# A four-layer graph kernel: first tile of each attention step searched from its bare guess, one adjacency product moved into the step change, side pairs over other rounds

## The reference

```python
for s in range(STEPS):                      # 2 steps
    A = _adj_from_feats(Xa, W1, W2, W3)     # softmax, nucleus 0.9, softmax again
    Xf = Rf @ Xf
    Xb = Rb @ Xb
    Xa = A @ Xa
    Z = Z + (Xf @ U1[s] + Xb @ U2[s] + Xa @ U3[s])
```

## Time and profile before

| | |
|---|---|
| median of 3 runs | 3476.09 us (3475.62 to 3479.3) |
| the profiled execution | 3477.54 us |
| its span | 3475.8 us |
| TensorE busy, granted clock | 3141.6 us (90%), 0.958 |
| VectorE busy | 2449.9 us (70%) |
| ScalarE busy | 1598.2 us (46%) |
| POOL busy | 2154.7 us (62%) |
| exact-loop rounds (MAX8) | 74 |

### The profile page before, as it was taken

One profiled execution on the slowest core, in us unless ns is written; L12 is line 12 of the kernel. 1 busy time (PEld: TensorE's weight loads), 2 busy tenths in 40 slices (PEclk: granted clock), 3 DMA queues, 4 the chain that ended last, 5 costly groups with the idle time before them and its releaser, 6 DMA issues. The chain is left out here.

```text
span 3475.8 us, 42043 instructions
## 1 busy us (share of the span) xinstructions
PE 3141.6 (90%) x13212; PEld 2270.6 (65%) x13212; DVE 2449.9 (70%) x3401; ACT 1598.2 (46%) x2357; POOL 2154.7 (62%) x4214
## 2 busy tenths in 40 slices
PE   4999989997799999999976689988899999996899
PEld 3888778885567777777754255544566666664788
DVE  6840123333998889888883799999988999998000
ACT  2311322225666666666653445545555555652100
POOL 2212421114788888888881677878988788886211
PEclk9999999998899999999988899999999999998899
DMA  7644344433112222122111111211222222233255
GB/s 254 241 146 145 116 151 167 165 130 87 44 54 59 61 63 60 57 60 64 57 37 58 47 56 53 57 48 51 58 82 75 78 80 82 74 87 99 96 197 173
DMA packets 140702, 327.59 MB, mean 94 GB/s; under 512 B 15456, under 2 KB 93664, under 8 KB 129248
## 3 DMA queue, kind: packets, MB, share of 16 engines
q1 hardware_dynamic: 140512, 325.30, 29.5%
HBM read 286.70 MB, written 38.54 MB: 94 GB/s over the span
## 5 line engine op out<-in xcount | busy, mean ns | idle before, releaser
L1025 ACT ACTIVATE junk<-E,negp 128x3327 uint8<-128x3327 f32 x208 | 637.3, 3064 | 141.3 <-issue 107.3
L1397 DVE SCALAR_TENSOR_TENSOR U<-E,trial 128x3327 f32<-128x3327 f32 x182 | 678.1, 3726 | 0.0
L920 PE MATMUL bank<-big,adj 128*128 128x512 f32 x1352 | 608.7, 601 | 8.7 <-ACT t L1051 8.7
L920 PEld LDWEIGHTS bank<-big,adj 128*128 128x128 f32 x1352 | 252.4, 192 | 328.9 <-issue 327.9
L297 PE MATMUL bank<-big,E 128*128 128x256 f32 x1664 | 366.7, 382 | 2.8 <-PEq L58 1.7
L880 PE MATMUL bank<-Hc,PT 128*128 128x256 f32 x1248 | 303.1, 395 | 65.5 <-ACT PT L1064 65.4
L880 PE MATMUL bank<-Hc,adj 128*128 128x256 f32 x1456 | 338.0, 384 | 16.4 <-ACT adj L1064 16.2
L297 PEld LDWEIGHTS bank<-big,E 128*128 128x128 f32 x1664 | 315.8, 191 | 50.3 <-issue 5.7
L1359 DVE TENSOR_REDUCE nmax<-E 128x1 f32<-128x3327 f32 x52 | 188.0, 3615 | 208.8 <-ACT E L1068 208.8
L880 PEld LDWEIGHTS bank<-Hc,adj 128*128 128x128 f32 x1456 | 279.5, 193 | 79.8 <-issue 22.5
L880 PEld LDWEIGHTS bank<-Hc,PT 128*128 128x128 f32 x1248 | 244.3, 198 | 126.3 <-ACT PT L1064 77.0
(11 more groups left out here) (248 smaller groups left out, 5750.2 us busy)
## 6 DMA issues: line engine op xcount, KB each, us to landing
adj<-adjT SPq DMA_DIRECT2D x131, 448.0 KB, 3.4
E<-adjT SPq DMA_DIRECT2D x32, 1664.0 KB, 6.9
adj<-adjT SPq DMA_DIRECT2D x104, 384.0 KB, 3.3
adj<-adjT SPq DMA_DIRECT2D x20, 1664.0 KB, 7.0
E<-adjT SPq DMA_DIRECT2D x26, 1216.0 KB, 5.8
xt<-xin SPq DMA_DIRECT2D x52, 128.0 KB, 5.8
x_d<-xn SPq DMA_DIRECT2D x52, 128.0 KB, 1.7
xt<-x_d SPq DMA_DIRECT2D x52, 128.0 KB, 5.3
```

Source lines behind the costliest of these rows:

```text
L920: last = mm(agg[:, 0:w], adj[:, SPAN * (k % 2) + j - AGG[k]], rhs[:, j], start=(j == 0), stop=False)
L1025: go(junk[:, 0:N], E[:, t % DEPTH, 0:N], func, bias=negp[:, t % 2, j:j + 1], scale=1.0, accum_out=acc_[:, t % 2, j:j + 1]).then_inc(summed ...
L1397: V_.scalar_tensor_tensor(out=U[:, 0:N], in0=e, scalar=point, in1=e, op0=ALU.is_ge, op1=ALU.mult, accum_out=found))
```

## The change

Four things change.

1. Tiles 0 and 26 (`unaided(t)`: t % NT == 0) have no ScalarE passes and no POOL updates. The guess, without the shift, is written as the first point at once and `bracketed` is raised. VectorE searches the tile right behind the next tile's maximum, a round earlier than the others, with 4 evaluations in step one and 5 in step two (`ALONE`). ScalarE's first copy of the tile after next waits for `bracketed` there, since that copy's sums overwrite what the guess reads.
2. `KEEP_END` of step two is 0.85 instead of 0.75, for all its tiles.
3. Step two's first product stands in round 27, the others in round n + 5 (LATE = 5): rounds 32 to 56. In rounds in which scores are made and nothing is turned (`filling`: 0 to 3 and 31 to 34), all four parts of the product come behind the four slots.
4. The 13 side pairs stand in rounds 45 to 48, 50 to 52 and 54 to 59 (`PAIRS`). Where a round has no product, SP loads both blocks of the pair itself; the loads for the last layer stay in round 59 (CLOSE = 7).

```diff
@@ -17,6 +17,7 @@
 EVALS = (3, 4)
+ALONE = (4, 5)
...
-KEEP_END = (0.8, 0.75)
+KEEP_END = (0.8, 0.85)
...
-LATE = 7
+LATE = 5
+CLOSE = 7
+PAIRS = (0, 1, 2, 3, 5, 6, 7, 9, 10, 11, 12, 13, 14)
...
-            side_at = lambda i: i - (NT + LAG + FIRST + 7) if 0 <= i - (NT + LAG + FIRST + 7) < NT // 2 else None
+            side_at = lambda i: PAIRS.index(i - (NT + LAG + FIRST + 7)) if i - (NT + LAG + FIRST + 7) in PAIRS else None
...
+            unaided = lambda t: t % NT == 0
+            aided = lambda t: t - 1 - t // (NT + 1)
...
-            agg_at = lambda i: i if 0 <= i < NT else i - LATE if NT <= i - LATE < tiles else None
+            agg_at = lambda i: i if 0 <= i < NT else NT if i == NT + 1 else i - LATE if NT < i - LATE < tiles else None
...
-            spread = [b for i in range(rounds + 1) for b in [last_at(i)] if b is not None and i < tiles + LATE]
+            spread = [b for i in range(rounds + 1) for b in [last_at(i)] if b is not None and i < tiles + CLOSE]
...
+                        def load_side(v, k):
+                            to = SPAN * k
+                            sp.dma_start(adj[:, to:to + FIRST], adjT[2 * v + k, :, 0:FIRST]).then_inc(side_in[k], 16)
...
                             if v is not None:
+                                if n is None:
+                                    for k in range(2):
+                                        load_side(v, k)
                                 for k in range(2):
                                     sp.wait_ge(side_done[k], v + 1)
-                                    load_chunk(n + 1, k)
-                            if i == tiles + LATE:
+                                    if n is not None and n + 1 < tiles:
+                                        load_chunk(n + 1, k)
+                            if i == tiles + CLOSE:
...
+                            filling = L is not None and T is None
...
-                                if n is not None:
+                                if n is not None and not filling:
+                                    neighbours(n, k)
+                            if n is not None and filling:
+                                for k in range(SLOTS):
                                     neighbours(n, k)
...
                                     act.wait_ge(lg_done, SLOTS * L + k + 1)
+                                    if k == 0 and L >= 2 and unaided(L - 2):
+                                        act.wait_ge(bracketed, L - 1)
...
-                                if k == 0 and R is not None:
+                                if k == 0 and R is not None and not unaided(R):
                                     sums(R, 1, 0)
...
-                                 ts(ga_(8), ga_(5), 1.0, -SHIFT[step], ALU.mult, ALU.add))
+                                 ts(ga_(8), ga_(5), 1.0, 0.0 if unaided(t) else -SHIFT[step], ALU.mult, ALU.add))
...
-                            offer(t, 0)
+                            if not unaided(t):
+                                offer(t, 0)
...
-                            prepare(t)
+                            if unaided(t):
+                                then(ts(trial2[:, d, POINT:POINT + 1], p, 1.0, None, ALU.mult))
+                                pool.sem_inc(bracketed, 1)
+                            else:
+                                prepare(t)
...
-                            for k in range(EVALS[step]):
+                            for k in range(ALONE[step] if unaided(t) else EVALS[step]):
...
                             if F is not None:
                                 row_max(F)
-                            if S is not None:
+                                if unaided(F - 1):
+                                    find(F - 1)
+                            if S is not None and not unaided(S):
                                 find(S)
```

More of the change, by code:

```diff
@@ L820, in _ @@
                                     elif v is not None:
-                                        to = SPAN * (k - 2)
-                                        sp.dma_start(adj[:, to:to + FIRST],
-                                                     adjT[2 * v + k - 2, :, 0:FIRST]).then_inc(side_in[k - 2], 16)
+                                        load_side(v, k - 2)
                                     elif n + 1 < tiles:
@@ L1015, in sums @@
                         def sums(t, j, m):
+                            a = aided(t)
                             if m == 0:
-                                act.wait_ge(aimed[j], t + 1)
+                                act.wait_ge(aimed[j], a + 1)
                                 if j > 0:
-                                    act.wait_ge(summed[j - 1], PASSES[j - 1] * (t + 1))
-                                elif t >= 1:
-                                    act.wait_ge(summed[1], 2 * t)
+                                    act.wait_ge(summed[j - 1], PASSES[j - 1] * (a + 1))
+                                elif a >= 1:
+                                    act.wait_ge(summed[1], 2 * a)
                             else:
-                                act.wait_ge(summed[j], 2 * t + 1)
+                                act.wait_ge(summed[j], 2 * a + 1)
                             func, acc_ = ((ACT.Relu, over), (ACT.Sign, sign))[m]
@@ L1099, in _ @@
                                         go(h3o[:, W % 2], dense[:, 0:D], ACT.Copy).then_inc(h3_copied, 1)
-                                if k == 3 and F is not None:
+                                if k == 3 and F is not None and not unaided(F):
                                     sums(F, 0, 1)
@@ L1123, in _ @@
                                         go(junk_y[:], y[:, X % 2], ACT.Copy, accum_out=stat[:, X % 2, 0:1]).then_inc(ln_a, 1)
-                                    if R is not None:
+                                    if R is not None and not unaided(R):
                                         sums(R, 1, 1)
@@ L1140, in _ @@
                                            accum_out=stat[:, X % 2, 2:3]).then_inc(ln_a, 1)
-                                    if F is not None:
+                                    if F is not None and not unaided(F):
                                         sums(F, 0, 0)
@@ L1245, in update @@
                             count, mass_ = up_(5 + j), up_(8 + j)
-                            pool.wait_ge(summed[j], PASSES[j] * (t + 1))
+                            pool.wait_ge(summed[j], PASSES[j] * (aided(t) + 1))
                             then(ts(count, sign[:, q, j:j + 1], 0.5, N / 2, ALU.mult, ALU.add))
```

## The result

| | before | after |
|---|---|---|
| median (5 runs each) | 3475.75 us (3473.58 to 3479.3) | 3491.74 us (3488.35 to 3494.7) |
| the profiled execution | 3477.54 us | 3493.73 us |
| its span | 3475.8 us | 3491.9 us |
| exact-loop rounds (MAX8) | 74 | 72 |

The ratio of the times is 1.0046, with a 95% interval from 1.0035 to 1.0057: slower, by less than half a percent. The forecast was 3466 us; the time lies inside the range (3433 to 3493), on the other side of no change.

A forecast was written before the change was run, and what follows sets the result against it. TensorE was taken to bound step one and 2434.7 to 3083, VectorE step two's first half and the last searches. 3477.54 + 6 + 0 + 4 - 20 = 3467.5, less 1.45 to the median: 3466 us; range over cases 3433 to 3493.

The forecast's parts named there:

- Part one: Fill of step one: search 0 starts earlier, search 1 5.4 us later, TensorE 6.2 later; +6, carried to step one's end.
- Part four: TensorE-bound stretch and drain: fewer pairs, earlier end of products and less idling give some -20; last search ends near 3196.
- signs of being wrong: MAX8 not 74 in all; search 1 earlier than 895; turn 26 before 1995; round 28 ending past 1862.
- The extra 12 of round 45: First round with a side pair, 12 us over: a stall that may stay or go, taken as 6, bounds 0 and 12.
- The 3.6 us that VectorE idles before search 51: In the drain: this idling goes, since the round feeding that bracket has no product any more; 3.6 us gained.
- The two pairs' 8: Rounds 49 and 53: leaving out two pairs before round 57 gives TensorE 10.2 us, of which about 8 remains.
- Parts two and three: Step change, product in round 27: 0, bounds +5 and -3. Fill of step two: search 28 4 us later, +4.
- Factor 0.85: Step two's searches: costs nothing itself, direction of the 45 rounds unknown; taken as 0, bounds 19 rounds fewer or as many more.
- Rival 1: Tiles 0 and 26 and the new factor: bare guesses cost extra exact-loop rounds, 8.9 us each; three more give 3493; chance 0.23.
- Rival 2: Step two's searches: the factor saves exact-loop rounds, three fewer in all, giving 3439; chance 0.22.
- Rival 3: Step two: all TensorE's moved work comes off, two rounds' products (48.8) and two pairs (10.2), giving 3417; chance 0.04.
- Rival 4: Nothing is left: round 45's 12 us stay and the step change costs its 5, giving 3477; chance 0.08.

The follow-up runs named there:

- e4: Kernel before with only the moved products (27, 32 to 56) and the change's side pairs: 3479.82 us against 3475.88, ratio 1.0012.
- e10: Kernel before plus bare searches with tile t+2's maximum inside, factor 0.85, products in rounds n + 6 (26 in 27), old pairs: 3431.97 us against 3475.81.
- e12: e10 with the change's rounds for the side pairs as the only edit: 3433.93 us against 3476.93, ratio 0.9876 to the kernel before.
- e3: Kernel before with the factor 0.85 alone: 3469.18 us against 3475.88, ratio 0.9977.
- e2: Kernel before with the fill order alone (rounds 0 to 3, 33, 34: score slots first, then the product): 3487.48 us against 3475.88.
- e8: Kernel before with product 26 in round 27, the others in rounds n + 6, side pairs as before: 3474.17 us against 3479.63.
- e6: Kernel before with bare searches alone, tile t+2's maximum taken inside the bare search: 3446.08 us against 3479.63, ratio 0.9904.
- e1: Kernel before with the bare searches of tiles 0 and 26 alone: 3481.45 us against 3475.88, ratio 1.0019.
- e7: e2 plus three unread matmuls behind each of the first three score slots of rounds 0 to 3: 3487.89 us against the kernel before's 3479.63.

## Why the prediction was wrong

**What held.** Search 26 starts 28 us earlier against its surroundings (1905 for 1932.68 predicted: 27.7), and its search ends 21.8 earlier (22.5). Search 27 gains 3.3 (3; the count of 21 us from exponential to search that Part one makes gives 1990 and a gain of 1.6, so the match is partly luck). Less the 12.8 of step one, the turn of tile 26 is at 2006.7 (2006), and search 28 3.8 late (4). Exponential 2 started after 875 and right behind search 0. MAX8 is 72, not 74, one of the signs of being wrong; so is the end of round 28 (turn 25 at 1867.07, where 1862 was the limit), which is step one's loss carried on. (Part four's 3196 for the end of the last search leaves out step one's +6; the sum has it.)

**Part four: predicted -20, measured -2.8** (from +19.6 to +16.8). This step is 17 of the 26 us by which the forecast missed. What failed in it is the premise that from 2434.7 to 3083 TensorE sets the pace, read from busy shares of 632.7 and 599.4 in 648.3 us. VectorE's waits for other engines in the kernel before, over that window, are (us in total, times, longest)

```profile
DVE nmax L1359 <- ACT E L1068: 24.4, 4, 10.3
...
DVE sc L1395 <- POOLq L1274: 0.6, 1, 0.6
```

and the last of the four is

```profile
2624.32 3.62 DVE L1359 TENSOR_REDUCE nmax<-E 128x1 f32<-128x3327 f32 x1 [6.38 <-ACT E L1068]
```

From there to the end of search 50 at 3160 the searches stand back to back on VectorE. Work taken from TensorE in rounds 49 and 53 can't end them earlier, and e4 shows it: turn 49 comes 8 us less late, search 49 only 0.7. In its own terms:

- *The extra 12 of round 45, taken at 6.* It is 61.1 us as before (2498.46 to 2559.53), and the 8.72 us wait for `t L1067` is in it. The row of it was already in the earlier trace rows ("8.7 <-ACT t L1051 8.7"): ScalarE's copy that frees the bank stands behind a normalisation copy, which waits for a POOL result. It is 8.7 in all fourteen kernels. The prediction saw a shift of 4 us "against POOL and ScalarE", but everything came to that round shifted together (turn 36, with which it starts, and search 37, beside it, are both 19.6 late here, and equal to within 0.1 us in every kernel), so nothing acted on this wait, and it was the bound 0 that held. Whether a shift of one engine against the others would remove it wasn't tried.
- *The 3.6 us that VectorE idles before search 51 "go".* They went, and 7.83 us in front of search 50 took their place (at 3136.03, above). POOL's timeline there:

```profile
3111.53 4.10 POOL L1318 TENSOR_TENSOR xn<-xn 128x256 f32<-128x256 f32 x1
...
3118.34 0.57 POOL L1231 TENSOR_TENSOR ga<-Zs,known 128x1 f32<-128x1 f32 x1
...
3124.79 3.48 POOL L1251 TENSOR_SCALAR trial<-trial 128x1 f32<-128x1 f32 x1
...
3135.51 0.33 POOL L1296 TENSOR_SCALAR trial<-up,ends 128x1 f32<-128x1 f32 x1
```

  The bracket stands behind the whole guess of tile 51 and the layer norm's steps on POOL, which are nearly back to back from 3105.86 to 3136.03. That round has no product in it here, while e10 has one there and waits 3.05 us at the same place, so the product, which the prediction blamed for such a wait, is not what this one hangs on: it grows as search 49 comes earlier (e12 against e10). In e4, where search 49 comes only 0.7 us less late than search 44, the 3.6 us shrink to 1.0 and no other wait takes their place.
- *The two pairs' 8.* On TensorE they were right: the turn of tile 49 goes from +19.4, at tile 41, to +8.9. Search 49 followed with +6.2, but only because the factor had left VectorE room: of the 13.4 us that it gains on search 44, 8.4 are there in e3 too, without the pairs, and in e4, without the factor, it gains 0.7. Search 50 then waits for POOL, and the gain ends there. In this kernel tile 50 also has one round more by the factor (8.9). e12, with both kernels at two rounds there, shows the pairs' worth alone: nothing.

**Part one: predicted +6, measured +12.8,** of which 2.1 come before the first scores. The step that failed is "it needs maximum 1 (starts 827.37)": the same part lets TensorE's rounds grow from 19.6 to 25, yet kept that maximum's start. It is 5.7 late. Behind it the count on ScalarE was nearly right: from exponential 2 to search 1 21 us were predicted (880 to 901) and 22.8 measured. The second and third fill rounds are 27.6 and 27.3 us, not 25, and on their own (e2) delay search 0 by 15.3: the fill order was the largest single loss of the four, and the prediction gave it no line of its own.

**Parts two and three: predicted 0 and +4.** The turn of tile 25 has +2.4 over step one's share, inside the bounds of +5 and -3. Step two's fill gave 3.8 at search 28 and 3 more by search 30: together 6.8.

**Factor 0.85: predicted 0, measured -7** (e3). Its bounds held, and its rounds fell by two. In the whole change the one that paid in e3, tile 27's, lies in the 14.40 us that VectorE waits for maximum 30 and saves nothing.

**Rivals.** Rival 1 gave 3493 and the measured time is 3491.74, but by another cause: MAX8 fell, so the guesses were not dear. Rival 2 was right in direction and saw its saving inside the loss. Rival 3's mechanism, all of TensorE's moved work coming off, is not borne out: e12 shows no gain by the pairs, e4 a loss. The Trainium skill (Perfetto Trace Analysis, "Identifying Performance Opportunities") says that interleaving regimes with different busiest engines may help; the runs agree only for the move by one round (e8: -2.5 at the last search), while the move by two with the pairs gave +3.9. Rival 4 came nearest to what Part four did.

**What the prediction missed** is how large that one sentence was ("maximum 2 now stands behind that search"). It priced the delay as a side effect to bear, against a gain of 16 to 28 us on the search, and didn't ask what the change would be without it: e6 against e1.

## What to carry to other kernels

When a long operation is moved forward on an in-order engine, list what it now stands in front of, and for the shortest of these that feeds another engine look for a place inside the long one; here a 3.6 us maximum, twice, was worth 35 us. Two engines can both be over 90% busy in a stretch: which one sets the pace is read from who still waits for another there, not from the larger share. A wait doesn't change by a shift that all engines share; before counting on its going, name the engine that moves against the others. A gain on one engine near a drain ends at the next wait for another queue, so follow it to the last instruction before it goes into the sum.

## What the runs showed of the hardware

POOL's small operations stretch beside one kind of VectorE pass. The operation over 128x1 at 3124.79 took 3.48 us where its like take 0.19 to 0.57, and it ended with VectorE's pass over two inputs (L1467, 3124.59 for 3.61); the operation at 3111.53 took 4.10 instead of 0.73, beside VectorE's cut (L1427, 3110.83 for 4.22). While VectorE ran MAX8 and MATCH_REPLACE, from 3115.89 to 3124.29, POOL did 21 operations of 0.19 to 0.73 us. By the Trainium skill (SBUF — State Buffer, "SBUF: two separate sides") POOL and a VectorE operation with two SBUF inputs take the shared ports as an exclusive lock for a whole instruction. The trace agrees. What it costs here wasn't measured by a run of its own.

TensorE's clock in the fill follows what it did before. In the window from 799.5 to 916 of the kernel after the granted clock is 0.83. A score group of the same form takes 0.92 us at 819.60, close behind a product, and 1.65 us behind the waits for ScalarE of 2.69 us at 823.58 and of 17.12 us at 892.90. e7 got half of the short ones back, and search 0 came no earlier.
